# Row fetches taken off GpSimd: single rows by SyncE's queue in eight gather stages, by ScalarE's queue too in two of them

## The reference, cut to what matters

```python
# three pooling layers
p = segment_max(h[src], dst)            # the largest neighbour row, per node
x = relu(concat([x, p]) @ Wm.T + bm)    # layers 2 and 3 with a residual and a layer norm
# three attention layers
score = (q[dst] * k[src]).sum(-1) / 16  # softmax over the edges of a node, then the sum of v[src]
# a sum by relation (2 kinds of edge), then gates and a small MLP
s = segment_sum(message[type2, src], dst)
# a sum by relation (8 kinds of edge), divided by the degree
s = segment_sum((h @ W[type8])[src], dst)
```

## Time and profile before

| What | us |
|---|---|
| median of the runs | 4991.76 |
| lowest and highest run | 4986.15, 7978.92 |
| the profiled execution, own time | 4998.77 |
| its span, first to last instruction | 4996.9 |

### The profile page before, as it was taken

How to read it: one execution, slowest core, us unless ns; L and a number is a source line. 1 busy time by engine, 2 the same in 40 slices (tenths; PEclk the granted TensorE clock), 3 DMA queues, 4 the chain that set the end, 5 groups by cost and what they waited for, 6 DMA issues and landing times.

```text
span 4996.9 us, 64715 instructions
## 1 busy us (share of the span) xinstructions
PE 2990.6 (60%) x15422; PEld 2152.1 (43%) x15422; DVE 2844.5 (57%) x8700; ACT 1726.9 (35%) x4725; POOL 3230.1 (65%) x3289
## 2 busy tenths in 40 slices
PE   3121189967899788888888888788800007961100
PEld 2011167756777665556555565556700003431000
DVE  6755344445444788877888788787443331124433
ACT  1000069955789443335333353333400003420000
POOL 4767667766767377774777747775067772027776
PEclk7555589988899899999999999999955558985555
DMA  5656566656666433333333333333166662246665
GB/s 179 199 170 218 190 210 224 220 190 193 201 213 221 136 103 105 104 104 96 102 104 104 103 94 103 104 105 95 43 228 205 209 204 88 101 146 205 207 205 190
DMA packets 280170, 776.97 MB, mean 155 GB/s; under 512 B 64641, under 2 KB 103810, under 8 KB 275842
## 3 DMA queue, kind: packets, MB, share of 16 engines
q0 software_dynamic: 157104, 429.21, 30.7%
q1 hardware_dynamic: 122706, 343.62, 18.0%
HBM read 455.64 MB, written 316.93 MB: 155 GB/s over the span
## 4 chain that ended last, share of the span: by engine, by line
PE 25%; POOL 14%; DMA 11%; issue 8%; DVE 5%; ACT 2%; DVEq 1%; POOLq 0%; ACTq 0%; SPq 0%
POOL HC L508 11%; PE PS L1314 8%; PE PS L1306 5%; PE PS L1240 3%; DMA X<-table,idx_src 3%; PE PS L1008 3%; DMA HC<-table,idx_src 3%; DMA HC<-table_typ,run_typ 2%; DMA HC<-table_rel,run_rel 2%; POOL HC L484 2%; POOL X L484 1%; DVE work L1931 1%; PE PS L1295 1%; PE PS L1403 1%; DVE W L1923 1%
## 5 line engine op out<-in xcount | busy, mean ns | idle before, releaser
L1744 DVE SCALAR_TENSOR_TENSOR HC<-HC,run_rst 128x256 f32<-128x256 f32 x1890 | 917.6, 486 | 1195.0 <-DMA HC<-table,run_max 526.0
L508 POOL DMA_INDIRECT HC<-table,run_max x1113 | 1098.1, 987 | 450.7 <-issue 305.5
L484 POOL DMA_INDIRECT HC<-table,idx_src x648 | 643.7, 993 | 352.4 <-DMA table<-B 155.8
L1115 PE MATMUL PS<-AM,ring 128*128 128x256 f32 x3000 | 731.0, 401 | 102.2 <-ACT ring L718 63.4
L484 POOL DMA_INDIRECT X<-table,idx_src x600 | 602.7, 1004 | 182.9 <-issue 127.7
L1115 PEld LDWEIGHTS PS<-AM,ring 128*128 128x128 f32 x3000 | 585.1, 200 | 247.9 <-DVE HC L1744 101.1
L1306 PE MATMUL PS<-AM,work 128*128 x3744 | 651.6, 285 | 22.0 <-DVE score L1931 20.5
L1987 DVE SCALAR_TENSOR_TENSOR HC<-HC,fcol,PS 128x257 f32 x1248 | 586.2, 470 | 102.6 <-PE PS L1314 93.2
L508 POOL DMA_INDIRECT HC<-table_typ,run_typ x391 | 378.7, 968 | 394.6 <-DMA table_typ<-HC 275.7
L1148 PE MATMUL PS<-ident,HC 128*128 128x128 f32 x10 | 3.4, 444 | 1002.4 <-DVE HC L1744 1002.4
L508 POOL DMA_INDIRECT HC<-table_rel,run_rel x391 | 378.1, 967 | 289.1 <-DMA table_rel<-AM 170.3
(11 more groups left out here) (261 smaller groups left out, 4390.2 us busy)
## 6 DMA issues: line engine op xcount, KB each, us to landing
prefix<-HC SPq DMA_DIRECT2D x485, 512.0 KB, 3.3
table_typ<-HC SPq DMA_DIRECT2D x18, 1024.0 KB, 3.8
HC<-table,run_max POOLq DMA_INDIRECT x1113, 3.2
HC<-table,idx_src POOLq DMA_INDIRECT x648, 2.8
X<-table,idx_src POOLq DMA_INDIRECT x600, 2.8
HC<-table_rel,run_rel POOLq DMA_INDIRECT x391, 2.8
HC<-table_typ,run_typ POOLq DMA_INDIRECT x391, 2.8
table_typ<-AM SPq DMA_DIRECT2D x6, 1024.0 KB, 3.8
```

The lines of the kernel that those rows point to most:

```text
L484: pool.indirect_dma_start(held(t)[:, 0:D], None, table, bass.IndirectOffsetOnAxis(ap=idx_src[:, t:t + 1], axis=0)).then_inc(landed[t % AHE ...
L508: pool.indirect_dma_start(run_slot(k), None, src, bass.IndirectOffsetOnAxis(ap=run_idx[s[1]][:, j:j + 1], axis=0)).then_inc(landed[k], 16)
L1115: last = nc.tensor.matmul(PS[:, (2, 5)[c % 2], 0:D], quads[:, (QUADS * x + g) % 4, b % 4, :], A[:, b, :], start=(b == 0), stop=(b == BLOCK ...
L1744: V.scalar_tensor_tensor(run_slot(k), run_slot((j - 1) % SLOTS), run_rst[:, j:j + 1], fresh, fade, join).then_inc(pooled, 1)
```

## The change

Three new lists take tiles and steps away from GpSimd: `BY_SP` (7 tiles of each pool and sum), `BY_ACT` (7 more tiles, sums only), `LONE` (8 steps of each attention layer). Each such tile of 128 rows is fetched by 128 DMAs of one row of 1 KB. The issuing engine loads 32 indices at a time into registers (`BITE`) and issues a DMA whose source address comes from a register. SyncE issues 10 of them in each turn (`A_TURN`) from turn 1 on, before that turn's wait and write; in attention 43 after each `row_in` load (`A_CHUNK`). ScalarE issues all its rows at the head of the sum stages. The rows go to buffers of their own (three for SyncE's and two for ScalarE's in use at a time), so GpSimd leaves those tiles out. VectorE waits on `x_in[...]` (or `far_in`) for them.

Index lists come from a new input `singles`; in the sums, SyncE loads two of its lines at the stage's head, after it has waited for the table, and VectorE forms the table's row numbers from them (`singles_known`) before tile 0. In attention the indices of the eight steps are written once to HBM (`step_idx`) and loaded into `far_src`, two ahead.

```diff
+BY_SP = [65 + 51 * i for i in range(7)]
+BY_ACT = [67 + 51 * i for i in range(7)]
+BITE = 32
+A_TURN = 10
+LONE = [56 + 48 * i for i in range(8)]
+A_CHUNK = 43
+def fetched_in(s):
+    return [] if s[0] != "runs" else BY_SP if s[1] == "max" else BY_SP + BY_ACT
...
+        spare = sb("spare", [P, 2, ROW])
...
+        def fetch(eng, n, rows, js, free):
+            s = PLAN[n]
+            for i, j in enumerate(js):
+                if i >= free:
+                    eng.wait_ge(pooled, before(n, ("runs",)) * TILES + js[i - free] + 1)
+                for p in range(0, P, BITE):
+                    regs = nc.values_load_multi_w_load_instructions(
+                        single_src[s[1]][0:1, bass.ds(fetched_in(s).index(j) * P + p, BITE)], engines=(eng.engine,), min_val=0,
+                        max_val=rows.shape[0] - 1, skip_runtime_bounds_check_because="the indices are the graph's own")[1]
+                    for k in range(BITE):
+                        eng.dma_start(single_home(s, j)[p + k:p + k + 1, :], rows[bass.ds(regs[k], 1), :]).then_inc(x_in[single_sem(j)], 16)
+                        yield
+        def fetch_lone(eng, n):
+            layer = PLAN[n][1]
+            for i, t in enumerate(LONE):
+                eng.wait_ge(x_in[3 + i % 2], 16 * (1 + layer * len(LONE) // 2 + i // 2 + 1))
+                if i >= 2:
+                    eng.wait_ge(attended, layer * STEPS + LONE[i - 2] + 1)
+                for p in range(0, P, BITE):
+                    regs = ...
+                    for k in range(BITE):
+                        eng.dma_start(held(t)[p + k:p + k + 1, 0:D], table[bass.ds(regs[k], 1), :]).then_inc(far_in[i % 3], 16)
...
 GpSimd, attention
+                        if t in LONE:
+                            continue
 GpSimd, runs
-                        if j in picked_in(s):
+                        if j in picked_in(s) + fetched_in(s):
                             continue
 SyncE, runs
+                    if s[1] != "max":
+                        kind = 1 if s[1] == "rel" else 2
+                        sp.dma_start(single_src[s[1]], singles[0:1, :]).then_inc(loaded, 16)
+                        sp.dma_start(single_type.bitcast(I32), singles[kind:kind + 1, :]).then_inc(loaded, 16)
+                    one_by_one = fetch(sp, n, {"max": table, "rel": table_rel, "typ": table_typ}[s[1]], BY_SP, 3)
                     for g in range(TURNS):
...
+                        elif g == 1:
+                            sp.wait_ge(singles_known, 1 if s[1] == "rel" else 2)
+                        if g >= 1:
+                            for _ in range(A_TURN):
+                                next(one_by_one, None)
 SyncE, attention
+                    lone = fetch_lone(sp, n)
                     for c in range(NCHUNK):
...
                         sp.dma_start(row_in[:, c % 2], step_rows[c * CHUNK:(c + 1) * CHUNK]).then_inc(rows_in[c % 2], 16)
+                        for _ in range(A_CHUNK):
+                            next(lone, None)
 ScalarE, head of both sums (the counterpart of "rel" stands for "typ")
+                    act.wait_ge(singles_known, 1)
+                    for _ in fetch(act, n, table_rel, BY_ACT, 2):
+                        pass
 VectorE, runs
+                    if not most:
+                        dve.wait_ge(loaded, 16 * (9 if s[1] == "rel" else 11))
...
+                        V.tensor_copy(single_src["rel"], single_f).then_inc(singles_known, 1)
...
+                        elif j in fetched_in(s):
+                            g = j // 4
+                            dve.wait_ge(written[g % TEAMS], 16 * (drained(n, g % TEAMS) + g // TEAMS))
+                            dve.wait_ge(x_in[single_sem(j)], x_count(n, single_sem(j), j))
+                            fresh = single_home(s, j)
```

More of the change, by code:

```diff
@@ L103, in picked_in, with gnn_kernel @@
     return PICKED if s[:2] == ("runs", "max") and s[2] > 1 else []
-def gnn_kernel(nc, edges, runs, picks, xN, weights, biases, bias_rows, out, table, table_rel, table_typ, stash, step_rows, prefix):
+def fetched_in(s):
+    return [] if s[0] != "runs" else BY_SP if s[1] == "max" else BY_SP + BY_ACT
+def gnn_kernel(nc, edges, runs, picks, singles, xN, weights, biases, bias_rows, out, table, table_rel, table_typ, stash, step_idx, step_rows, prefix):
     PLAN = plan()
@@ L394, in columns, with x_count @@
         def columns(s, k, upto=TILES):
-            return sum(1 for j in range(k, upto, SLOTS) if j not in picked_in(s)) if k < SLOTS else 0
+            return sum(1 for j in range(k, upto, SLOTS) if j not in picked_in(s) + fetched_in(s)) if k < SLOTS else 0
+        def x_count(n, k, j=-1):
+            return 16 * sum({"start": 1, "attention": (s[-1] == LAYERS - 1) + (len(LONE) // 2 if k >= 3 else 0), "runs": P * sum(1 for f in fetched_in(s) if single_sem(f) == k)}.get(s[0], 0)
+                            for s in PLAN[:n]) + 16 * P * sum(1 for f in fetched_in(PLAN[n]) if single_sem(f) == k and f <= j)
         def own_bank(s, b):
@@ L414, in landings @@
         def landings(n, k):
-            return (before(n, ("attention",)) * len(range(k, STEPS, AHEAD))
+            return (before(n, ("attention",)) * sum(1 for t in range(k, STEPS, AHEAD) if t not in LONE)
                     + sum(columns(s, k) + (1 if k < BLOCKS else 0) for s in PLAN[:n] if s[0] == "runs"))
@@ L442, in part, with lone_in @@
             return G[:, bass.ds(b, 1), a, :].rearrange("p o d -> p (o d)")
+        def fetch(eng, n, rows, js, free):
[17 more added lines that the diff above has]
+                for p in range(0, P, BITE):
+                    regs = nc.values_load_multi_w_load_instructions(
+                        far_src[0:1, i % 3, p:p + BITE], engines=(eng.engine,), min_val=0, max_val=NODES - 1,
+                        skip_runtime_bounds_check_because="the indices are the graph's own")[1]
+                    for k in range(BITE):
+                        eng.dma_start(held(t)[p + k:p + k + 1, 0:D], table[bass.ds(regs[k], 1), :]).then_inc(far_in[i % 3], 16)
+                        if p + k == P - 1 and i + 2 < len(LONE):
+                            eng.dma_start(far_src[0:1, (i + 2) % 3, :], step_idx[i + 2:i + 3, :]).then_inc(x_in[3 + i % 2], 16)
+                        yield
+        def lone_in(n, i):
+            return 16 * (far_before(n, i % 3) + P * (PLAN[n][1] * len(range(i % 3, len(LONE), 3)) + i // 3 + 1))
         def block_regs(eng, s, count=RING):
@@ L606, in _ @@
                         sp.dma_start(step_rows.rearrange("(c q) a e -> q c a e", q=P), rows4).then_inc(stored, 16)
+                        with nc.allow_non_contiguous_dma(reason="one index a row, once"):
+                            sp.dma_start(step_idx.rearrange("c p -> p c"), idx_src[:, LONE[0]::AHEAD][:, 0:len(LONE)]).then_inc(stored, 16)
                     if s[1] == "max":
@@ L992, in _ @@
                     act.sem_inc(stage_done, 1)
+                elif s == ("runs", "typ"):
+                    begin(act, n)
+                    act.wait_ge(singles_known, 2)
+                    for _ in fetch(act, n, table_typ, BY_ACT, 2):
+                        pass
         @block.tensor
@@ L1928, in score_of @@
                         dve.wait_ge(expanded, t0 + t + 1)
-                        dve.wait_ge(landed[k], 16 * (landings(n, k) + t // AHEAD + 1))
+                        if t in LONE:
+                            dve.wait_ge(far_in[LONE.index(t) % 3], lone_in(n, LONE.index(t)))
+                        else:
+                            dve.wait_ge(landed[k], 16 * (landings(n, k) + t // AHEAD + 1))
                         dve.wait_ge(scored, t0 + t)
@@ L2075, in picked_rows, with single_rows @@
     return np.ascontiguousarray(rows[2][:, PICKED].T)
+def single_rows(rows):
+    import numpy as np
+    return np.ascontiguousarray(rows[2:5, :, BY_SP + BY_ACT].transpose(0, 2, 1).reshape(3, -1))
 def kernel(**inputs):
@@ L2126 @@
     runs, picks = put("runs", by_run), put("picks", picked_rows(by_run))
-    args = [e, runs, picks, put("xN", xN), [put(f"w{i}", v) for i, v in enumerate(w)], put("bias_in", bias), put("bias_rows", rows)]
+    singles = put("singles", single_rows(by_run))
+    args = [e, runs, picks, singles, put("xN", xN), [put(f"w{i}", v) for i, v in enumerate(w)], put("bias_in", bias), put("bias_rows", rows)]
     args.append(nc.dram_tensor("outN", (P, BLOCKS, D), F32, kind="ExternalOutput").ap())
```

46 lines of the change are left out of this document (40 added, 6 removed).

## The result

| What | us |
|---|---|
| before, median of 4 runs beside the kernel after | 4988.95 |
| after, median of 4 runs (5275.32 to 5279.14) | 5277.52 |
| ratio after / before, 95% interval | 1.0578 (1.0563 to 1.0593) |
| span of the profiled execution after | 5276.9 |

The forecast was 4910 us. The loss is 289 us where a gain of some 80 was named. One of the four runs of before, 7978.92 us, is left out of the ratio, as is one of `e11_none`, 8466.70 us. I write e5 for `e5_static`, and so on. In some of them before takes 4987 to 4988 us, as here; I call these sessions at 4988. In others it takes 5944 to 6013 us. Each result is held against before in its own session.

The account below looks back on a forecast made before the run. GpSimd's fetches were taken as the bound: 73 fewer gave 94.5 us, less 7 lost in pool 2, so 87.5 off 4998.8, 4911, stated as 4910 us (1.6%). Own range 4900 to 4955; 8 in 10, 4894 to 5100.

Parts of the forecast that it names:

- the price of a row: Issuing queue's time per one-row DMA, c: 0.42 us taken, near prices 0.40 to 0.48; SyncE's turn 10c + 0.32 + 0.05.
- rival A: SyncE becomes the pace, slower: at c = 0.50 a sum of -164 us, 5163 us; chance 0.24.
- lags less 15 us: Run stages: SyncE's deficit over 90 turns, less 15 us hidden before GpSimd stops, as writes are due six turns later.
- The turning point at 10 rows a turn, c = 0.47: Rival A: row price at which the change turns from gain to loss; over 2% slower from 0.49 on.
- Attention: Attention layers: SyncE's 18.4 us a chunk against 20.4, covered by 2.0 us; 8 fetches fewer each, 31.3 us gained.
- The 14 steps of early arrival: Attention: a lone step's last row goes out about 14 steps before it is scored; cover of 15 us in rival A.
- The ceiling: All stages: 73 fetches less at their whole period, 94.5 us, 1.9% of the span; 4904 us.
- GpSimd as the pace: Fetch stages: GpSimd's busy time plus 0.305 us issue per fetch fills the window, so each fetch saved gains its period.
- Full to the last microsecond in seven of the eight stretches: GpSimd's busy plus issue time equals the window in seven fetch stretches, nearly in the first pool (518.5 of 532.0).
- The sums' head: Sums' start: index loads and VectorE passes bring tile 0 8 to 15 us later, costing nothing under the 30 us ring.
- Rival B: One DMA engine is the pace, 0.23 us a row: about +530, 5530 us; chance 0.06 with the sums' doubling of c.
- Rival C: Attention does not follow, TensorE and VectorE being the pace there: 31 us go, 4942 us; chance 0.12.

Follow-up runs that it names:

- e11_none: Kernel after with nobody fetching the 73 tiles and steps, like e17; its kind, with before at 5957, 6013 and 6006 us: 0.9843, 0.9871, 0.9859 of before.
- e5_static: Kernel after with source rows fixed when the program is written, no register loads or address arithmetic, same 9344 one-row transfers: 4961.68 us, 0.9946 of before.
- e17: Kernel after with nobody fetching or waiting for the 73 tiles and steps, index loads and step_idx write kept: 4921.41 us, 0.9862 of before.
- e2_fewer: Kernel after with 5 SyncE tiles a stage at 7 rows a turn, 6 attention steps at 32 a chunk; before at 5944.3: 6377.4 us, 1.0732.
- e6_fewer: Same edit to the kernel after as e2_fewer, in a session at 4988: 4938.77 us, 0.9898 of before.

## Why the prediction was wrong, and where it was right

**The step that failed is the price of a row.** "I take 0.42, near the low end, because the 16-row load is the nearest row" fell by three terms. The DMA itself was rated high enough: 0.228 us, not 0.282. The arithmetic was 0.037 for 0.046. But there is a move beside it that the sum did not have (29 ns, and a gap with each instruction, so that 0.294 us of instructions become 0.410); the register load is the upper of the two values weighed, 0.066 and not 0.035; and in the run stages issues and loads are stretched now and then, which brings the mean to 0.515. The choice of the low end, by likeness to a bigger transfer, was the mistake: a transfer with a register address differs in its instructions, and these were priced in the earlier trace rows, not in the earlier trace rows.

**The mechanism was rival A's, as written.** With c = 0.515 its working gives turns of 5.52 us, 5.80 in pools 2 and 3: lags less 15 us of 2, 93, 80 and twice 42, net a gain of 7.5 in pool 1, and losses of 84, 70 and 24 twice. Measured: 9.9 lost, 76.8, 60.4, 33.2 and 26.5. Pool 1 is 17 us off this working, and why is open; the others are within 10. Its marks are there, rows over 0.47 us apart and GpSimd at `prefix<-HC`. The turning point at 10 rows a turn, c = 0.47, was not measured; that a turn of SyncE longer than GpSimd's is what decides rests on the kernels with 10 and with 7 rows a turn, and on the one with cheap issues.

**Attention was the second miss.** At 0.50 rival A took 9 us net a layer for it, and the forecast had it covered by 2.0 us a chunk. Measured with all that SyncE issues it is 63.5 us for 48 steps, 21.2 a chunk of 16, against 20.4, and each layer cost 21 to 24 us against before (10 to 11 in the window, 10 to 12 behind it). The 14 steps of early arrival that should have taken up 15 us did not exist: they assumed that VectorE comes to a single step at the mean pace of the layer, and 45 steps in 49 us, 1.09 each, had shown that it does not at the start; SyncE starts its rows late besides, as seen above.

**The ceiling** of 94.5 us was 86.6 in the windows, 66 in the medians and 71 between the profiled spans; the write of `step_idx` was not in the sum. **GpSimd as the pace** was right in the main: with the rows gone, each stage shortened by its fetches times their period, to within 4 us. "Full to the last microsecond in seven of the eight stretches" was a misreading: in pool 3 the same sum gives 348.99 + 361 x 0.305 = 459.1 of 474.7 us, and that pool gave 5.9 us in e17 where 9.2 were forecast. **The sums' head** cost nothing that shows in e17's windows; the 2.3 and 4.1 us ahead of them are not assigned. **Rival B** did not happen in the kernel after, its price of 0.23 us a row was nearly four times the 0.063 measured, and its symptom showed behind A in `e5_static`. **Rival C** did not hold.

The chances put 0.24 on A and the range ended at 5100; its working reaches 5100 at c = 0.49. The measured 0.515 lay outside the bounds from the near rows, since these counted two instructions and one gap for a row that has three of each, and no stretched issues.

## What to carry to other kernels

Work moved to an idle queue is paid for in instructions, and a thin cover makes a cliff: past the point where that queue becomes the pace, each hundredth of a microsecond a row costs, by the working above, 90 turns x 10 rows x 0.01 = 9 us in each of pools 2 and 3. Before moving, count every instruction of one item (registers, moves, gaps, the transfer) and leave the new queue room for its price to be a quarter higher (0.515 for 0.42 here); here 7 rows a turn won 1% and 10 lost 6%. And take due dates from the fastest stretch of the consumer, not from its mean.

## What the runs showed of the hardware that I had not expected

- A register load's time is nearly in proportion to its registers: 1.105 us for 16 on TensorE's queue, 2.12 us for 32 on SyncE's, that is 66 to 69 ns each; 2.77 us for 32 on ScalarE's in the sums.
- One-row DMAs from two queues at a steady 3.8 a us leave a 512 KB write's landing at 3.4 us; in bursts, at a mean of 4.3, it is 13.8 us at the median (`e5_static`).
- A write of 1024 single words of 4 bytes (768 in `e2_fewer` and `e6_fewer`), issued ahead of them, holds the first fetched rows up by 9 to 11 us.
- A DMA issue of one row, 228 ns at the median, takes over 0.4 us in 5 to 6% of SyncE's cases in the run stages and never in the attention layers (278 ns at most). What stretches it is open.
- In the sessions where the kernel before takes 5944 to 6013 us, queues with many small instructions suffer most: 43 rows 32 us against 20, and e6's edit, 1% faster at 4988, is 7% slower there. A kernel with no rows gains 1.3 to 1.6% in both. Why the instructions of one queue stand 0.70 us apart in some stretches there, and what sets the sessions apart, is not settled.
